# A mixture of experts that adds its rows into one tensor in memory instead of two in turn

## The reference, cut to what matters

```python
x = _layernorm(x + _L0_attn_ref(x, ...), axis=-1)
x = _layernorm(x + _L0_ffn_ref(x, ...), axis=-1)      # 8 experts, each token to one
x = _layernorm(x + _L1_attn_ref(x, ...), axis=-1)
x = _layernorm(x + _L1_ffn_ref(x, ...), axis=-1)      # 16 experts, each token to four
```

```python
combine = jnp.sum(jax.nn.one_hot(topi, E) * topw[..., None], axis=2)
def body(acc, expert):
    w1e, b1e, w2e, b2e, ce = expert
    hmid = jax.nn.gelu(x @ w1e + b1e, approximate=False)
    return (acc + (hmid @ w2e + b2e) * ce[:, None], None)
```

## Time and profile before

| | |
|---|---|
| median of 3 runs | 2240.51 us (2233.95 to 2241.57) |
| the profiled execution's own time | 2247.24 us |
| its span in the profile | 2245.5 us |
| TensorE busy | 1721.8 us, 77% of the span |
| GpSimd busy | 626.6 us |
| second experts' stage, first scatter's start to last scatter's start | 1651.34 to 2184.70 us |
| last join, first load to the end | 2193.01 to 2245.5 us |

### The profile page before, as it was taken

The page is one execution under the profiler, slowest core; times in us unless marked ns, Lnnn a source line. Parts: engine busy times, 40 slices in busy tenths (PEclk is TensorE's granted clock), DMA queues, the critical chain, the costliest instruction groups (busy, mean ns, idle before and its releaser), DMA issues. The chain is left out here.

```text
span 2245.5 us, 33537 instructions
## 1 busy us (share of the span) xinstructions
PE 1721.8 (77%) x9958; PEld 1166.6 (52%) x9959; DVE 1259.9 (56%) x2016; ACT 1043.2 (46%) x2189; POOL 626.6 (28%) x598
## 2 busy tenths in 40 slices
PE   4889887542998298869999999043389999999980
PEld 1333333541897254423444443043279999999980
DVE  6999995757111622178888882396923333333326
ACT  5777775410232232127777775010435555555540
POOL 0000000020564000011111111312067776777753
PEclk9999998555899599959999996555589999999995
DMA  3000000650220964253433330647234444444419
GB/s 117 1 0 1 0 19 38 218 178 3 63 65 26 328 216 159 75 81 77 92 81 90 90 86 11 239 131 251 72 91 70 70 70 68 71 65 69 67 18 299
DMA packets 164488, 211.44 MB, mean 94 GB/s; under 512 B 30483, under 2 KB 119966, under 8 KB 164256
## 3 DMA queue, kind: packets, MB, share of 16 engines
q1 hardware_dynamic: 122784, 137.07, 20.6%
q0 software_dynamic: 41600, 73.08, 14.7%
HBM read 132.74 MB, written 83.23 MB: 96 GB/s over the span
## 5 line engine op out<-in xcount | busy, mean ns | idle before, releaser
L1238 PEld LDWEIGHTS f_ht_ps<-f_XT,f_WS 128*128 128x128 f32 x2944 | 360.8, 195 | 18.6 <-issue 5.8
L1238 PE MATMUL f_ht_ps<-f_XT,f_WS 128*128 128x128 f32 x2944 | 366.9, 279 | 3.0 <-ACT f_XT L1279 3.0
L1246 PE MATMUL f_y_ps<-W,f_HT 128*128 x1472 | 348.1, 380 | 0.0
L1801 DVE TENSOR_REDUCE att_MX<-att_s_ps 128x2 f32<-128x1024 f32 x256 | 305.1, 1220 | 70.2 <-PE att_s_ps L1680 69.1
L1202 POOL DMA_INDIRECT moe<-f_Y,TOK x184 | 280.0, 1522 | 186.3 <-ACT f_Y L1304 143.7
L1783 ACT ACTIVATE att_PT<-att_st_ps 128x512 f32<-128x512 f32 x512 | 278.3, 596 | 101.5 <-PE att_st_ps L1705 90.7
L1246 PEld LDWEIGHTS f_y_ps<-W,f_HT 128*128 128x128 f32 x1472 | 265.7, 190 | 28.7
L1331 DVE COPY f_WS<-W 128x1024 f32 x184 | 136.0, 740 | 215.6 <-PE f_ht_ps L1238 131.4
L303 PE MATMUL rec_gate<-rec_XC,rec_W 128*128 128x512 f32 x384 | 187.8, 642 | 68.4 <-ACT rec_R L205 42.8
L1705 PE MATMUL att_st_ps<-att_Q,att_K 50*128 50x512 f32 x512 | 224.7, 503 | 19.5 <-ACT att_PT L1783 17.2
L1339 DVE TENSOR_TENSOR f_Y<-f_y_ps,f_B 128x256 f32<-128x256 f32 x144 | 61.1, 425 | 294.2 <-PE f_y_ps L1246 294.2
(11 more groups left out here) (228 smaller groups left out, 2397.8 us busy)
## 6 DMA issues: line engine op xcount, KB each, us to landing
W<-in_w POOLq DMA_DIRECT2D x48, 512.0 KB, 13.4
x<-n_Y SPq DMA_DIRECT2D x24, 512.0 KB, 4.5
n_X<-x SPq DMA_DIRECT2D x24, 512.0 KB, 8.7
n_Y<-moe SPq DMA_DIRECT2D x24, 512.0 KB, 8.8
att_Q<-qk_pairs SPq DMA_DIRECT2D x192, 64.0 KB, 3.0
att_K<-qk_pairs SPq DMA_DIRECT2D x192, 64.0 KB, 3.1
qk_pairs<-prj_HI SPq DMA_DIRECT2D x16, 512.0 KB, 3.3
qk_pairs<-prj_LO SPq DMA_DIRECT2D x16, 512.0 KB, 5.1
```

The lines of the kernel that those rows point to most:

```text
L1238: mm = nc.tensor.matmul(ht_ps[r % 2][:, f * P:(f + 1) * P], WS[r % 2][:, at:at + P], XT[r % 2][:, c], start=(c == 0), stop=(c == DC - 1))
L1246: mm = nc.tensor.matmul(y_ps[r % 2][:], HT[r % 2][:, f], W2[:, bass.ds(e * W_EXPERT + f * D, D)], start=(f == 0), stop=(f == FC - 1))
L1801: nc.vector.tensor_reduce(MX[n % 2][:, qc, :, p], s_ps[m % 2][:], AX.X, ALU.max).then_inc(s_mx, 1)
```

## The change

The second experts' stage gets one accumulator, and each scatter waits for the landing of the one just ahead of it. The routing stage therefore zeroes one tensor, and the last join reads one tensor less and has no addition of the two on GpSimd. The first experts' stage is as it was.

```diff
             def scatter(n):
-                if K > 1 and n >= 2:
-                    pool.wait_ge(s_sc[(n - 2) % R], 16 * ((n - 2) // R + 1))
+                if K > 1 and n >= 1:
+                    pool.wait_ge(s_sc[(n - 1) % R], 16 * ((n - 1) // R + 1))
                 pool.wait_ge(s_y, n + 1)
                 settle()
@@
-    moe1 = [dram(f"moe1_{k}", (T, D)) for k in range(2)]
+    moe1 = [dram(f"moe1_{k}", (T, D)) for k in range(1)]
```

## The result

| | before | changed |
|---|---|---|
| median | 2238.88 us (4 runs, 2233.95 to 2241.57) | 2350.65 us (4 runs, 2340.13 to 2354.6) |
| span of the profiled execution | 2245.5 us | 2352.9 us |
| scatter 0 to scatter 136 | 509.37 us | 625.48 us |
| scatter 136 to the last | 23.99 us | 24.30 us |
| last join, first load to the end | 52.5 us | 43.8 us |

The changed kernel is slower: ratio 1.0479, 95% interval 1.0451 to 1.0506. The profiled spans differ by 107.4 us. Of these the run of real tiles holds +116.1 (625.48 - 509.37) and the last join -8.6; what is left (-0.1) is the last eight tiles and the stages ahead.

What follows compares the result with a forecast made beforehand. It took TensorE's 3.73 us per tile to bound the stage before, and landing plus release after. 123.0 + 0.9 - 7.1 = +116.8 us on 2247.24 us gives 2364.0, less 6.7 to the median: 2357 us, range 2325 to 2395 us.

Steps and rivals of the forecast that it cites:

- The bound moves to the chain of landing and release: Second experts' stage: scatter, landing, next scatter becomes the bound, 4.65 us a step against TensorE's 3.73 us.
- The landing is the scatter's own: Second experts' stage: scatters don't disturb one another, so landing stays 3.8 us, 2.7 without rows plus 1.1 for 128 rows.
- The release of 0.85 us: GpSimd's time from a landing to the next scatter's start, taken from two waits ahead of indexed transfers; lower end 0.29 us.
- Rival 1: Second experts' stage: release takes 0.29 us as for a plain transfer, step 4.09 us, time 2280 us; chance 8%.
- +123.0 us for the real tiles: Scatters 1 to 136 of the second experts' stage: 136 steps of 4.65 us, 632.4 us in place of 509.4.
- The last eight tiles, +0.9: Seven steps behind scatters without rows: 2.7 + 0.85 = 3.55 us each, 24.9 us in place of 24.0.
- The join, -7.1 us: Last join: second sum 5.4 us sooner, and six steps at 4.5 us each save 1.7 us more.
- Zero stores, 0: Routing stage: eight zero stores fewer gain nothing, since 51 us of cover hide them before and after.
- The clock: TensorE in the second experts' stage: about 80% busy, with its clock staying at 1.00.
- rival 3: TensorE's clock falls in the second experts' stage; with half the tiles at half clock, 2554 us; chance 4%.
- Rival 2: Second experts' stage: landing shrinks to 2.9 us or less, the wait is free, only the join gains, 2233 us; chance 5%.

## Why the prediction was right, point by point

- **The bound moves to the chain of landing and release.** Right. Landing 3.80 us expected, 3.79 in the mean over the 136 real tiles; TensorE waits for gathers. The run with the wait alone and the run with overwriting scatters show it from both sides.
- **The landing is the scatter's own.** Right: 3.8 us with neighbours 3.73 or 4.60 us apart. Of the two parts (2.7 us without rows, 1.1 us for rows) the second fell to 0.6 with half rows. Both are those of an adding scatter alone: an overwriting one with all its rows lands in 2.4 us.
- **The release of 0.85 us.** The number was near, 0.79 us measured, but the reason that I gave for it was wrong. The two rows it was taken from have the register instruction behind the wait, as the new wait has; that is why they fitted, not that they stand at an indexed transfer. In so far the number was luck. The value of 0.27 us that a plain transfer shows is reached by the indexed one, for the wait on a landing, as soon as that instruction is moved. Rival 1 (quick release, 2280 us) was thus a true possibility of this kernel, one line away, and ended at 2292 us for another reason, the copies.
- **+123.0 us for the real tiles.** Measured +116.1. The release is 0.06 us shorter, 8.7 us over 136 tiles; landing and release alone give 4.57, and the step of 4.60 holds 0.03 us more, mostly five starts that come 1.1 to 1.6 us behind the landing.
- **The last eight tiles, +0.9.** Measured +0.3.
- **The join, -7.1 us.** Measured -8.6. I took 4.5 us for a step, from a row of before that I held for undisturbed (2222.61 to 2227.13). It was not: a GpSimd addition ran there from 2223.74 to 2226.08 and met the start of the normalising, which took 1.56 us. Without the additions it takes 1.38 us and the step 4.34, which is 1.0 us more over six steps. The first sum came 4.7 us sooner, not 3.9, and the second 6.0, not 5.4.
- **Zero stores, 0.** Right: with them (the run of the shorter join alone) the last join is as short.
- **The clock.** It stayed at 1.00 over the stage; rival 3 fell. TensorE's busy share is 89% and not 80%. One part is the beginning: TensorE goes at its own pace until it needs gathers that the held-up scatters hold back, some 24 tiles. But from 1750 to 2185 us it is still 379.08 of 435.00 us, 87%: a tile's matmuls are recorded as 4.0 us of busy time where they were 3.75 before (a transpose is 296 ns in the mean against 273 over 1661 to 2185 us, and the busy times of the three matmul lines overlap by 0.32 us a tile, where before, from 1750 to 2150 us, they overlapped by 0.49). This changes nothing in the sum.
- **Rival 2** (a shorter landing, so that only the join's gain is left) did not come, and the run with overwriting scatters shows that its mechanism is right: at 2.4 us of landing the time is 2233 us, the number given.

The errors point the same way: 6.9 us too much for the tiles, 0.6 for the last ones, 1.5 too little gain in the join, 9.0 us together, where 116.8 was given for the profiled spans' difference and 107.4 measured. In medians 2357 us was given and 2350.65 measured.

## What to carry to other kernels

A wait on the transfer just ahead makes its time to landing plus the time to start again the least step of the loop; compare that sum with the pace of the engine that bounds the stage, and where it is larger by 0.85 us, as here, 136 tiles lose 116 us. One tensor less to read was worth 8.6 us, and it could be had without the wait, by letting one accumulator start as the input of the sum. Where a loop is bound by a wait and the instruction behind it, put register work ahead of the wait, and look in the trace whether it is gone from behind it: here it went for the landing (0.79 to 0.27 us) and not for ScalarE's rows (0.86 to 0.78 us).

## What the runs showed of the hardware beyond that

- A scatter with its register instruction behind the wait started 0.79 us after the landing it waited for; with it ahead, 0.27 us. Moved in all scatters, that gave 58 us of the 112 us back. Behind ScalarE's rows the start came 0.86 and, moved, 0.78 us after ScalarE's end.
- In the second experts' stage an adding scatter of 128 rows of 1 KB took 1.59 us to issue and 3.8 us to land, an overwriting one 1.0 and 2.4 us. The overwriting scatters of the first experts' stage took 1.32 and 2.8 us in the same run.
- VectorE's copy of the first weights from on-chip memory to on-chip memory, 0.69 us, held up scatters' issues: in the run with one accumulator and the register instruction ahead, 44 of 136 took over 1.75 us, up to 2.10, in place of 1.59. Of these 41 started within a copy, and none of the 41 was longer by more than what its copy still had to run: the one that started 0.06 us into a copy of 0.69 us took 2.09 us. With the two-input instruction, 1.23 us, 61 of 136 took over 1.75 us, up to 2.62. With the form that has an accumulator output, 1.22 us, none took over 1.63 us. Which of the issue's accesses to memory waited is not shown.
